# Expert stage: results stored with a partition's four tiles together, the last nine groups by GpSimd through row numbers

## The chip, the cores and the metric

One of the eight cores of a Trainium2 chip runs the program. TensorE multiplies matrices, VectorE (DVE), ScalarE (ACT) and GpSimd (POOL) work on tiles, SyncE (SP) issues DMAs; ACT and POOL issue DMAs too, and all of these run on the core's 16 DMA engines. The metric is the device time of the program in microseconds (us), the median of three runs.

## What is computed

10,000 nodes with 512 features go through two graph layers and two feed-forward layers, each with a layer norm and a residual sum. The change touches the last layer, a mixture of 64 experts in which each node takes two experts:

```
sel = route(x, hash_proj, 2)                # two experts of 64 for each node
pos = place of each (node, expert) pair within its expert; keep = pos < 1250
buf[expert, pos] = x of the kept pairs
h = gelu(buf @ W1[expert])                  # 512 -> 32
y = h @ W2[expert]                          # 32 -> 512
out = mean over the node's two picks of y[expert, pos] * keep
x = x + out
```

## The kernel before, in words

The kernel runs in stages, with a barrier of all engines between them: the projections of the first graph layer (79 tiles of 128 nodes), its edges, its combination with the first feed-forward layer, the edges and nodes of the second graph layer with the routing, the expert stage, and the combine stage. The order of the work is written out by hand for each engine; engines wait for one another by semaphores.

The routing gives every (node, expert) pair a slot, so that an expert's pairs stand together and each expert starts on a new tile of 128 slots. There are at most `LISTED` = 219 such tiles, in `NG` = 55 groups of four (the last has three). How many hold pairs depends on the data; with the given inputs, the choices worked out from the reference fill 188 tiles, 47 groups, and the rest of the list is empty. Slots without a pair have a row number beyond the bound, and the DMA leaves them out.

The expert stage (lines 2081 to 2252) takes the tiles in turn. GpSimd gathers a tile's 128 rows of 2 KB through row numbers into one of eight buffers `xg` (L2122; it waits until the tile eight before has been transposed). TensorE transposes the tile (`turn`, L154), VectorE copies it to `gT` (L2236), TensorE multiplies a group by the up-weights (L2144), ScalarE applies gelu (L2188), TensorE multiplies by the down-weights (L2156), VectorE copies the four results to one of three groups of buffers `yo` (`result`, L2243), and ScalarE's queue stores the group to the tensor `YL` in HBM, "slot_outputs" (`store`, L2193). SP loads the down-weights of each group (L1622); ScalarE copies the up-weights out of `w1all` (L2180), which SP loads at the start of the stage (L2109), behind a store of 128 zero rows (L2108) for which GpSimd clears `zrow` (L2118). VectorE's turn in group g is: copy the tiles of g, then the results of g-2; before the first result of a group it waits until the store that used the buffers three groups ago has landed. After groups 8, 10 and 12 it also works out the slots' row numbers of the first three batches of the next stage (`find`, L2214 to L2230, result `qs`).

In the combine stage (2255 to 2345) GpSimd gathers, for four tiles of 128 nodes at a time (a batch), the two slots' rows of each node out of `YL` (L2295), and VectorE adds them with their weights to the residual (L2334, L2338). VectorE finds the row numbers of a batch three batches ahead (L2311 to L2328); GpSimd waits for them and for the sums of the batch three before.

Of the kernel before, what the change touches and what calls it, by code (L numbers as in the profile page):

```python
# [8 lines left out]
F32 = mybir.dt.float32  # L9
# [28 lines left out]
LISTED = (2 * N + ME * (P - 1)) // P  # L38
DROPPED = 200000.0
# [23 lines left out]
def gnn_ffn(nc, x, xTt, src, dst, Wl, Wr, att, gbias, Wc0, b1c, W2e, b2e, WT, bG, hashp, M1, M2, out):  # L63
    ctx = ExitStack()
    with ctx:
# [32 lines left out]
        FS = nc.dram_tensor("flat_src", [FL + P], F32).ap()  # L98
        RRR = nc.dram_tensor("window_resets", [EP, 2 * P], F32).ap()
# [92 lines left out]
        def unrolled(n, steps):  # L192
# [13 lines left out]
        wl = sb("wl", [P, DK, D], F32, pa)  # L206
        ef = sb("ef", [EP, 2, EC], F32, pa)
# [35 lines left out]
        (c_pool, c_id, c_int, c_ef, c_pad, c_flat, c_win, c_ne, c_rr, c_tab, c_len, c_dg, c_dgm, c_mk, c_mkt, c_tr,  # L243
         c_kd, c_idx, c_st, h_oh, h_mm, h_deg) = (
            sem("i_" + n) for n in ("pool id int ef pad flat win ne rr tab len dg dgm mk mkt tr kd idx st oh mm deg").split())
# [11 lines left out]
        with nc.Block() as block:  # L257
            @block.sync
            def _(sp):
# [21 lines left out]
                sp.wait_ge(c_st, 48)  # L281
                for s in range(4):
                    sp.wait_ge(a_st[s], 16 * len(range(s, NT, 4)))
                    sp.wait_ge(a_sr[s], 16 * len(range(s, NT, 4)))
                    sp.wait_ge(a_sb[s], 16 * len(range(s, NT, 4)))

            @block.scalar
            def _(act):
# [40 lines left out]

                more = ((wc, Wc0), (wg, WT), (hp, hashp), (w2, W2e))  # L330
# [12 lines left out]
            def _(pool):  # L343
# [20 lines left out]
                pool.memset(mk[:], 0.0)  # L364
                pool.memset(zin[:, 0:XE], 0.0)
# [1172 lines left out]
        trow = sb("trow", [1, 4 * P], I32)  # L1538
        ids = sb("ids", [P, 2 * P], I32)
# [45 lines left out]
        idf = sb("idf", [P, 2, P], F32, pe_)  # L1585
        g_c = sem("g_c")
        g_ld, g_t, g_tr, g_rw, g_rw2 = (sem(n) for n in ("g_ld", "g_t", "g_tr", "g_rw", "g_rw2"))
# [36 lines left out]
        with nc.Block() as block:  # L1624
# [106 lines left out]
            def _(dve):  # L1731
# [227 lines left out]
                nc.vector.tensor_copy(trow[:], bank[0][0:1, 0:4 * P]).then_inc(g_rw, 1)  # L1959
                dve.wait_ge(g_ld, 32)  # L1960
# [3 lines left out]
                dve.wait_ge(g_rw, 2)  # L1964
            @block.tensor
# [121 lines left out]
        zrow = sb("zrow", [P, D])  # L2087
# [6 lines left out]
        p_ld, p_st = sems("p_ld", 8), sems("p_st", 3)  # L2094
# [287 lines left out]
```

## Time and profile before

| | |
|---|---|
| median of 3 runs | 2737.44 us (2734.61 to 2737.51) |
| span of the profiled execution | 2733.6 us (3.8 us below the median) |
| busy in the span: PE, DVE, ACT, POOL | 77%, 67%, 36%, 66% |
| expert stage | 2151.6 to about 2504 us |
| combine stage | 2504.6 to the end |

The engines' rows in the trace give a start and a duration; a number of tiles merged into one row is shown as "x4". In brackets stands how long the engine had been idle before, and what ended the wait. "issue" is time in which the engine waited for nothing that the profile shows. The DMA share is the sum of the packets' times over 16 engines, and can pass 1. The granted clock of TensorE is a fraction of 2.4 GHz.

### The profile page before, as it was taken

The numbers are of one execution on the slowest core, as the hardware profiler recorded it, in microseconds if no ns is written. First come the engines' busy times: TensorE is split into PE (matmuls) and PEld (weight loads), VectorE is DVE, ScalarE is ACT, GpSimd is POOL, SyncE is SP. The second block draws the span as 40 slices with busy tenths as digits, with TensorE's granted clock in tenths as the row PEclk, the third lists the DMA queues.
The fourth block names the chain that finished last, engine by engine and source line by source line (L and its number), as shares of the span: only waits on it lengthen the run. The fifth ranks groups of instructions, "written<-read, shape, count | busy, mean of one in ns | idle before, by whom it ended". The sixth has DMA issues, their size and how long they took to land. (4 is left out here: it accounts for less than half of the span.)

```text
span 2733.6 us, 43338 instructions
## 1 busy us (share of the span) xinstructions
PE 2118.0 (77%) x11528; PEld 1261.1 (46%) x11554; DVE 1837.2 (67%) x5188; ACT 988.2 (36%) x2224; POOL 1794.8 (66%) x2144
## 2 busy tenths in 40 slices
PE   8999999957787738999978969999998377774000
PEld 3444444435565526665644426666665244452000
DVE  4776776645555569999951116777777388886675
ACT  1111111115555515777773425555555122220000
POOL 3555555567777458887737755777777667664776
PEclk9999999978999959999999989999999599997555
DMA  5755555548999746888749976666664599996999
GB/s 198 232 190 178 191 184 182 193 147 271 307 314 312 258 154 193 256 260 262 238 180 324 409 285 211 214 220 215 212 214 138 179 342 371 366 338 242 371 383 360
DMA packets 331876, 689.90 MB, mean 252 GB/s; under 512 B 48217, under 2 KB 55347, under 8 KB 331505
## 3 DMA queue, kind: packets, MB, share of 16 engines
q1 hardware_dynamic: 220088, 404.15, 42.7%
q0 software_dynamic: 76720, 218.39, 24.5%
q10 hardware_dynamic: 34825, 64.59, 6.4%
q8 instruction: 96, 1.57, 0.2%
q14 instruction: 147, 1.20, 0.1%
HBM read 416.71 MB, written 287.44 MB: 258 GB/s over the span
## 5 line engine op out<-in xcount | busy, mean ns | idle before, releaser
L2122 POOL DMA_INDIRECT xg<-n_rows,ids x219 | 219.0, 1000 | 109.6 <-PE psum L154 61.6
L148 PE MATMUL psum<-wl,xT 128*128 128x512 f32 x632 | 288.8, 600 | 0.0
L148 PE MATMUL psum<-wg,yT 128*128 128x512 f32 x632 | 285.5, 595 | 0.0
L148 PE MATMUL psum<-wr,xT 128*128 128x512 f32 x632 | 284.1, 592 | 0.0
L337 ACT ACTIVATE xb<-xa,xsc 128x512 f32<-128x512 f32 x79 | 64.2, 814 | 480.3 <-POOL xsc L397 480.3
L384 POOL TENSOR_TENSOR ve<-mv,epst 128x1 f32<-128x1 f32 x79 | 51.1, 647 | 254.1 <-DVE mv L439 254.1
L1688 POOL DMA_INDIRECT slot_tokens<-sl x158 | 169.1, 1070 | 70.9 <-issue 66.9
L2295 POOL DMA_INDIRECT q<-slot_outputs,qs x158 | 167.8, 1062 | 72.3 <-issue 47.8
L154 PE MATMUL psum<-ident,xg 128*128 128x128 f32 x876 | 136.4, 294 | 92.9 <-DVE gT L2236 73.4
L148 PE MATMUL psum<-wc,x1T 128*128 128x264 f32 x632 | 162.8, 402 | 35.0 <-DVE hb L1231 27.4
L148 PEld LDWEIGHTS psum<-wr,xT 128*128 128x128 f32 x632 | 120.1, 190 | 151.2 <-issue 151.2
L1072 POOL TENSOR_TENSOR oc<-ta,ts 128x512 f32<-128x512 f32 x79 | 137.4, 1740 | 59.1 <-DVE ta L1196 31.2
L154 PEld LDWEIGHTS psum<-ident,xg 128*128 128x128 f32 x876 | 99.9, 148 | 161.3 <-issue 138.6
L148 PEld LDWEIGHTS psum<-wl,xT 128*128 128x128 f32 x632 | 115.0, 190 | 120.2 <-issue 120.2
L533 DVE SCALAR_TENSOR_TENSOR xl<-psum,rs,gb_b 128x512 f32<-128x512 f32 x79 | 59.2, 749 | 163.8 <-PE psum L148 163.8
L148 PEld LDWEIGHTS psum<-wg,yT 128*128 128x128 f32 x632 | 114.5, 191 | 114.1 <-issue 114.1
L2236 DVE COPY gT<-psum 128x512 f32<-128x512 f32 x219 | 141.2, 683 | 37.6 <-PE psum L154 37.6
L686 POOL DMA_INDIRECT gl<-xl_rows,idx x118 | 136.7, 1158 | 38.6 <-issue 32.8
L2243 DVE COPY yo<-psum 128x512 f32<-128x512 f32 x219 | 135.8, 682 | 32.5 <-PE psum L2156 26.1
L690 POOL DMA_INDIRECT gr<-xr_rows,idx x118 | 132.9, 1127 | 36.0 <-issue 30.8
L148 PE MATMUL psum<-hp,x3T 128*128 128x256 f32 x632 | 149.9, 380 | 2.5 <-ACT x3T L2046 2.5
L1330 PE MATMUL psum<-w,hT 128*128 128x512 f32 x316 | 148.7, 593 | 0.0
(323 smaller groups left out, 5316.5 us busy)
## 6 DMA issues: line engine op xcount, KB each, us to landing
slot_outputs<-yo ACTq DMA_DIRECT2D x54, 1024.0 KB
x_rows<-x SPq DMA_DIRECT2D x158, 256.0 KB, 3.2
edge_sums<-eo SPq DMA_DIRECT2D x29, 1056.0 KB, 6.5
edge_sums<-go SPq DMA_DIRECT2D x29, 1024.0 KB
xT<-in_xTt SPq DMA_DIRECT2D x79, 256.0 KB
xl_rows<-xl SPq DMA_DIRECT2D x79, 256.0 KB
xr_rows<-xr SPq DMA_DIRECT2D x79, 256.0 KB
residual_rows<-xb SPq DMA_DIRECT2D x79, 256.0 KB, 3.8
```

What stands on the lines that cost most here:

```text
L148: last = nc.tensor.matmul(ps, lhs[:, k, :], rhs[:, k, :], start=(k == 0), stop=(k == DK - 1))
L154: last = nc.tensor.transpose(ps[:, k * P:(k + 1) * P], rows[:, k * P:(k + 1) * P], ident[:])
L337: act.activation(xb[:, s, :], xa[:, s, :], ACT.Identity, scale=xsc[:, s, 1:2], bias=xsc[:, s, 0:1]).then_inc(a_xb, 1)
L686: pool.indirect_dma_start(gl[:, w % 16, :], None, XL, bass.IndirectOffsetOnAxis(idx[:, 0, w:w + 1], 0), bounds_check=NP - 1, oob_is_err=Fa ...
L690: pool.indirect_dma_start(gr[:, w % 8, :], None, XR, bass.IndirectOffsetOnAxis(idx[:, 1, w:w + 1], 0), bounds_check=NP - 1, oob_is_err=Fal ...
L1072: pool.tensor_tensor(oc[:, t % 3, :], ta[:, t % 3, :], ts[:, t % 3, :], ALU.add).then_inc(c_o, 1)
L1330: nc.tensor.matmul(bank[3 + 4 * h], hT[:, h, k, :], w2[:, k, :], start=(k == 0), stop=False)
L1688: pool.indirect_dma_start(IDXF, bass.IndirectOffsetOnAxis(sl3[:, k, t:t + 1], 0), sl3[:, 2, t:t + 1], None, bounds_check=ME * SLOTS * P - ...
L2122: pool.indirect_dma_start(xg[:, t % 8, :], None, XN3, bass.IndirectOffsetOnAxis(ids[:, t:t + 1], 0), bounds_check=NP - 1, oob_is_err=False ...
L2236: nc.vector.tensor_copy(gT[:, t % 8, :, :].rearrange("p k n -> p (k n)"), bank[t % 2]).then_inc(p_T, 1)
L2243: nc.vector.tensor_copy(yo[:, t % 12, :], bank[4 + t % 4]).then_inc(p_y, 1)
L2295: pool.indirect_dma_start(q0[:, b % 3, t % 4, k, :], None, YL, bass.IndirectOffsetOnAxis(qs[:, b % 3, t % 4, k:k + 1], 0), bounds_check=LI ...
```

## The change

The rows of `YL` get another order: the slot of partition p in tile t of group g was row 512 g + 128 t + p, and becomes row 512 g + 4 p + t. So one partition's four results of a group lie side by side, and a group's store has 128 rows of 8 KB where it had 512 of 2 KB. ScalarE's queue stores groups 0 to 45 in this way (`SURE` = 46). The last nine groups are stored by GpSimd, with an indirect DMA of one row number for each partition (`store_wide`); the row numbers `wide` are worked out at the end of the routing, and those of a group that begins behind the last tile in use lie beyond the bound, so that nothing is written. `YL` is declared at the top, the row of zeros moves behind the last group, and the row blocks from group 46 on are filled with zeros in the projection stage, by ten stores on ScalarE's queue. `find` takes the slot number apart with shifts and masks to get the new row, in the expert stage and in the combine stage.

```
--- before
+++ after
+NG = -(-LISTED // 4)
+NOROW = 4 * NG * P
+SURE = 46
...
+                    if 24 <= t <= 24 + 4 * (NG - SURE) and t % 4 == 0:
+                        g = SURE + (t - 24) // 4
+                        n = 4 if g < NG else 1
+                        act.dma_start(YL[4 * g * P:(4 * g + n) * P, :].rearrange("(t p) c -> p t c", p=P),
+                                      zrow[:].unsqueeze(1).to_broadcast([P, n, D])).then_inc(c_zr, 16)
...
+                pool.iota(first[:], [[4, -(-LISTED // 4) - SURE]], base=4 * SURE, channel_multiplier=0,
+                          allow_small_or_imprecise_dtypes=True)
+                pool.iota(where[:], [[P, -(-LISTED // 4) - SURE]], base=P * SURE, channel_multiplier=1,
+                          allow_small_or_imprecise_dtypes=True)
...
+                nc.vector.tensor_scalar(empty[:], first[:], incl[:, ME - 1:ME], None, ALU.is_ge).then_inc(g_em, 1)
+                dve.wait_ge(g_em, 1)
+                nc.vector.scalar_tensor_tensor(wide[:], empty[:], DROPPED, where[:], ALU.mult, ALU.add).then_inc(g_em, 1)
                 dve.wait_ge(g_ld, 32)
                 nc.vector.tensor_copy(idf[:], idr[:]).then_inc(g_t, 1)
...
             def _(sp):
-                sp.wait_ge(z_0, 1)
-                sp.dma_start(YL[LISTED * P:LISTED * P + P, :], zrow[:]).then_inc(z_st, 16)
                 sp.dma_start(w1all[:].rearrange("p e c -> p (e c)"), M1).then_inc(p_all, 16)
...
             def _(pool):
-                pool.memset(zrow[:], 0.0).then_inc(z_0, 1)
+                def store_wide(g):
+                    pool.wait_ge(p_y, tiles(g)[-1] + 1)
+                    pool.indirect_dma_start(YL.rearrange("(r j) c -> r (j c)", j=4),
+                                            bass.IndirectOffsetOnAxis(wide[:, g - SURE:g - SURE + 1], 0),
+                                            yo[:, 4 * (g % 3):4 * (g % 3) + 4, :].rearrange("p j c -> p (j c)"), None,
+                                            bounds_check=NG * P - 1, oob_is_err=False).then_inc(p_sw[g % 3], 16)
+
                 for t in range(LISTED):
...
+                    if t % 4 == 1 and t // 4 - 4 >= SURE:
+                        store_wide(t // 4 - 4)
+                for g in range(NG - 4, NG):
+                    store_wide(g)
...
                 def store(g):
                     n = len(tiles(g))
                     act.wait_ge(p_y, tiles(g)[-1] + 1)
-                    act.dma_start(YL[4 * g * P:(4 * g + n) * P, :].rearrange("(t p) c -> p t c", p=P),
+                    act.dma_start(YL[4 * g * P:4 * (g + 1) * P, :].rearrange("(p t) c -> p t c", p=P)[:, 0:n, :],
                                   yo[:, 4 * (g % 3):4 * (g % 3) + n, :]).then_inc(p_st[g % 3], 16)
...
-                    if g >= 3:
+                    if 3 <= g < SURE + 3:
                         store(g - 3)
...
-                    nc.vector.tensor_scalar_min(qs[:, b % 3, 0:n, :], qg[:, 0:n, :], float(LISTED * P)).then_inc(z_ix, 1)
+                    nc.vector.tensor_scalar_min(qn[:, 0:n, :], qg[:, 0:n, :], float(NOROW)).then_inc(z_n, 1)
+                    dve.wait_ge(z_n, b + 1)
+                    nc.vector.tensor_scalar(qp[:, 0:n, :], qn[:, 0:n, :], P - 1, 2, ALU.bitwise_and, ALU.logical_shift_left)\
+                        .then_inc(z_p, 1)
+                    nc.vector.tensor_scalar(qt[:, 0:n, :], qn[:, 0:n, :], 7, 3, ALU.logical_shift_right, ALU.bitwise_and)\
+                        .then_inc(z_p, 1)
+                    nc.vector.tensor_scalar(qo[:, 0:n, :], qn[:, 0:n, :], 9, 9, ALU.logical_shift_right,
+                                            ALU.logical_shift_left).then_inc(z_p, 1)
+                    dve.wait_ge(z_p, 3 * (b + 1))
+                    nc.vector.tensor_tensor(qp[:, 0:n, :], qp[:, 0:n, :], qt[:, 0:n, :], ALU.bitwise_or).then_inc(z_o, 1)
+                    dve.wait_ge(z_o, b + 1)
+                    nc.vector.tensor_tensor(qs[:, b % 3, 0:n, :], qp[:, 0:n, :], qo[:, 0:n, :], ALU.bitwise_or)\
+                        .then_inc(z_ix, 1)
...
                 def result(t):
                     g = t // 4
-                    if t % 4 == 0 and g >= 3:
+                    if t % 4 == 0 and 3 <= g < SURE + 3:
                         dve.wait_ge(p_st[g % 3], 16 * (g // 3))
+                    if t % 4 == 0 and g >= SURE + 3:
+                        dve.wait_ge(p_sw[g % 3], 16 * len(range(SURE + (g - SURE) % 3, g, 3)))
```

The combine stage's `find` is changed in the same way, and its gathers are bounded by `NOROW`. GpSimd's instructions in the expert stage, before (`xg` is the gathered tile, `n_rows` its source):

```order
L2118 MEMSET zrow 128x512
L2122 DMA xg<-n_rows,ids 128x512 x219
```

and after:

```order
L2153 DMA xg<-n_rows,ids 128x512 x202
L2145 DMA slot_outputs<-yo,wide 7072x2048
L2153 DMA xg<-n_rows,ids 128x512 x4
L2145 DMA slot_outputs<-yo,wide 7072x2048
L2153 DMA xg<-n_rows,ids 128x512 x4
L2145 DMA slot_outputs<-yo,wide 7072x2048
L2153 DMA xg<-n_rows,ids 128x512 x4
L2145 DMA slot_outputs<-yo,wide 7072x2048
L2153 DMA xg<-n_rows,ids 128x512 x4
L2145 DMA slot_outputs<-yo,wide 7072x2048
L2153 DMA xg<-n_rows,ids 128x512
L2145 DMA slot_outputs<-yo,wide 7072x2048 x4
```

The memset is gone; five of the nine wide stores stand between the last 17 gathers, four behind them. VectorE's instructions around the first find of the expert stage, before (`qg` is the slot number, `qs` the row number that GpSimd uses):

```order
L2243 COPY yo<-psum 128x512 x4
L2214 TENSOR_TENSOR qe<-iota,selk 128x512
L2220 TENSOR_TENSOR qj<-qe,cbase 128x512
L2226 TENSOR_REDUCE qf<-qj 128x8
L2228 TENSOR_TENSOR qg<-qf,plk 128x8
L2230 TENSOR_SCALAR qs<-qg 128x8
L2236 COPY gT<-psum 128x512 x4
```

and after:

```order
L2292 COPY yo<-psum 128x512 x4
L2249 TENSOR_TENSOR qe<-iota,selk 128x512
L2255 TENSOR_TENSOR qj<-qe,cbase 128x512
L2261 TENSOR_REDUCE qf<-qj 128x8
L2263 TENSOR_TENSOR qg<-qf,plk 128x8
L2265 TENSOR_SCALAR qn<-qg 128x8
L2267 TENSOR_SCALAR qp<-qn 128x8
L2269 TENSOR_SCALAR qt<-qn 128x8
L2271 TENSOR_SCALAR qo<-qn 128x8
L2274 TENSOR_TENSOR qp<-qp,qt 128x8
L2276 TENSOR_TENSOR qs<-qp,qo 128x8
L2283 COPY gT<-psum 128x512 x4
```

One small operation has become six, ahead of the copies of the next group's tiles.

## Rows read from the trace of the kernel before

**Rows 1.** Windows: us, busy time of PE, PEld, DVE, ACT, POOL, clock, DMA share, GB/s.

```profile
100.00:200.00 100.00, 100.00 (x283) 44.84 (x282) 71.86 (x133) 11.39 (x14) 53.29 (x85) 1.00 0.57 193
2259.00:2441.00 182.00, 139.83 (x1740) 90.83 (x1736) 154.15 (x248) 46.96 (x157) 124.58 (x126) 0.96 1.02 374
```

**Rows 2.** Timeline, VectorE's copies of the results: start us, us, instruction [idle before].

```profile
2259.29 2.48 DVE L2243 COPY yo<-psum 128x512 f32<-128x512 f32 x4 [0.43 <-PE psum L2156]
2264.90 2.48 DVE L2243 COPY yo<-psum 128x512 f32<-128x512 f32 x4 [0.43 <-PE psum L2156]
...
2329.28 2.48 DVE L2243 COPY yo<-psum 128x512 f32<-128x512 f32 x4 [2.90 <-DMA slot_outputs<-yo]
...
2441.49 2.48 DVE L2243 COPY yo<-psum 128x512 f32<-128x512 f32 x4 [1.28 <-PE psum L2156]
```

**Rows 3.** Waits from 2180 to 2440 us: who, for what, total us, times, longest.

```profile
DVE yo L2243 <- DMA slot_outputs<-yo: 6.3, 4, 2.9
PEld psum L154 <- DMA xg<-n_rows,ids: 1.8, 4, 0.8
```

**Rows 4.** DMA queues from 2360 to 2400 us: packets, MB, share of 16 engines.

```profile
q10 hardware_dynamic: 3773, 7.50, 48.6%
q0 software_dynamic: 2243, 6.21, 41.2%
q1 hardware_dynamic: 1436, 1.96, 13.8%
```

**Rows 5.** DMA queues from 2156 to 2166 us, while the up-weights load.

```profile
q1 hardware_dynamic: 183, 3.35, 78.9%
```

**Rows 6.** Timeline of VectorE, the end of one find in the combine stage.

```profile
2541.80 0.17 DVE L2326 TENSOR_TENSOR qg<-qf,plk 128x8 f32<-128x8 f32 x1
2542.00 0.17 DVE L2328 TENSOR_SCALAR qs<-qg 128x8 int32<-128x8 f32 x1
2542.08 2.77 DVE L2334 SCALAR_TENSOR_TENSOR q<-q,w,qx 128x512 f32<-128x512 f32 x4
```

**Rows 7.** Timeline, the start of the expert stage on GpSimd and SP.

```profile
2151.59 0.53 POOL L2118 MEMSET zrow<- 128x512 f32 x1 [6.43 <-POOLq L80]
2152.14 0.33 SPq L2108 DMA_DIRECT2D slot_outputs<-zrow  x1
```

**Rows 8.** Timeline, the end of the expert stage.

```profile
2455.64 1.00 POOL L2122 DMA_INDIRECT xg<-n_rows,ids  x1 [0.30 <-issue]
2457.33 1.00 POOL L2122 DMA_INDIRECT xg<-n_rows,ids  x1 [0.70 <-PE psum L154]
2458.31 2.48 DVE L2243 COPY yo<-psum 128x512 f32<-128x512 f32 x4 [0.43 <-PE psum L2156]
...
2479.76 1.00 POOL L2122 DMA_INDIRECT xg<-n_rows,ids  x1 [0.69 <-PE psum L154]
...
2489.58 0.63 PE L154 MATMUL psum<-ident,xg 128*128 128x128 f32 x4 [1.28 <-DVE gT L2236]
...
2497.75 0.69 DVE L2243 COPY yo<-psum 128x512 f32<-128x512 f32 x1 [0.32 <-PE psum L2156]
2498.47 0.36 ACTq L2193 DMA_DIRECT2D slot_outputs<-yo  x1
```

**Rows 9.** Timeline, small indirect DMAs before the expert stage, and who waits.

```profile
2139.58 0.97 POOL L1688 DMA_INDIRECT slot_tokens<-sl  x1 [0.30 <-issue]
...
2144.15 1.01 POOL L1726 DMA_INDIRECT idr<-slot_tokens,tid  x1 [0.31 <-issue]
...
2146.70 0.29 DVE L1961 CAST idf<-idr 128x256 f32<-128x256 int32 x1 [12.47 <-DMA idr<-slot_tokens,tid]
```

**Rows 10.** GpSimd's gathers of the combine stage: ns min/median/max, waits, and one gather.

```profile
L2295 POOL DMA_INDIRECT q<-slot_outputs,qs x158: 995/1002/1625, 2505.3 to 2719.4; - x158
its engine sat idle before it (us, times) until:
  issue: 47.8, 157
...
2541.50 1.00 POOL L2295 DMA_INDIRECT q<-slot_outputs,qs  x1 [0.30 <-issue]
```

More of the change, by code:

```diff
@@ L206, in gnn_ffn @@
         wl = sb("wl", [P, DK, D], F32, pa)
+        zrow = sb("zrow", [P, D], F32, pa)
         ef = sb("ef", [EP, 2, EC], F32, pa)
@@ L281, in _ @@
                 sp.wait_ge(c_st, 48)
+                sp.wait_ge(c_zr, 16 * (NG - SURE + 1))
                 for s in range(4):
@@ L364, in _ @@
                 pool.memset(mk[:], 0.0)
+                pool.memset(zrow[:], 0.0)
                 pool.memset(zin[:, 0:XE], 0.0)
@@ L1538, in gnn_ffn @@
         trow = sb("trow", [1, 4 * P], I32)
+        wide = sb("wide", [P, -(-LISTED // 4) - SURE], I32)
         ids = sb("ids", [P, 2 * P], I32)
@@ L1585, in gnn_ffn @@
         idf = sb("idf", [P, 2, P], F32, pe_)
+        first = sb("first", [P, -(-LISTED // 4) - SURE], F32, pe_)
+        where = sb("where", [P, -(-LISTED // 4) - SURE], F32, pe_)
+        empty = sb("empty", [P, -(-LISTED // 4) - SURE], F32, pe_)
         g_c = sem("g_c")
-        g_ld, g_t, g_tr, g_rw, g_rw2 = (sem(n) for n in ("g_ld", "g_t", "g_tr", "g_rw", "g_rw2"))
+        g_ld, g_t, g_tr, g_rw, g_em = (sem(n) for n in ("g_ld", "g_t", "g_tr", "g_rw", "g_em"))
         e_ld, e_lx, e_le, e_s3, e_sn, e_id = (
@@ L1964, in _ @@
                 dve.wait_ge(g_rw, 2)
+                dve.wait_ge(g_em, 2)
             @block.tensor
@@ L2078, in gnn_ffn @@
         end_phase(pe_)
-        YL = nc.dram_tensor("slot_outputs", [LISTED * P + P, D], F32).ap()
         qs = sb("qs", [P, 3, 4, 2], I32)
+        qn = sb("qn", [P, 4, 2], I32)
+        qp = sb("qp", [P, 4, 2], I32)
+        qt = sb("qt", [P, 4, 2], I32)
+        qo = sb("qo", [P, 4, 2], I32)
         qe = sb("qe", [P, 4, 2, ME], F32)
@@ L2093, in gnn_ffn @@
         phase.extend(p_w + p_v)
-        p_ld, p_st = sems("p_ld", 8), sems("p_st", 3)
+        p_ld, p_st, p_sw = sems("p_ld", 8), sems("p_st", 3), sems("p_sw", 3)
         p_all, p_cp = sem("p_all"), sem("p_cp")
-        z_eq, z_bs, z_f, z_ix, z_g, z_0, z_st = (sem("z_" + n) for n in "eq bs f ix g 0 st".split())
+        z_eq, z_bs, z_f, z_ix, z_g, z_n, z_p, z_o = (sem("z_" + n) for n in "eq bs f ix g n p o".split())
         p_tr, p_T, p_up, p_h, p_dn, p_y = (sem("p_" + n) for n in "tr T up h dn y".split())
-        NG = -(-LISTED // 4)
         def tiles(g):
@@ L2203, in _ @@
                 for k in range(3):
-                    act.wait_ge(p_st[k], 16 * len(range(k, NG, 3)))
-                act.wait_ge(z_st, 16)
+                    act.wait_ge(p_st[k], 16 * len(range(k, SURE, 3)))
+                    act.wait_ge(p_sw[k], 16 * sum(1 for g in range(SURE, NG) if g % 3 == k))
             @block.vector
@@ L2258, in gnn_ffn @@
         q_ld, q_x, q_st = sems("q_ld", 3), sems("q_x", 3), sems("q_st", 3)
-        q_eq, q_bs, q_f, q_g, q_ix, q_a, q_b = (sem("q_" + n) for n in "eq bs f g ix a b".split())
+        q_eq, q_bs, q_f, q_g, q_ix, q_a, q_b, q_n, q_p, q_o = (sem("q_" + n) for n in "eq bs f g ix a b n p o".split())
         with nc.Block() as block:
@@ L2327, in find @@
                     dve.wait_ge(q_g, b - 2)
-                    nc.vector.tensor_scalar_min(qs[:, b % 3, 0:n, :], qg[:, 0:n, :], float(LISTED * P)).then_inc(q_ix, 1)
+                    nc.vector.tensor_scalar_min(qn[:, 0:n, :], qg[:, 0:n, :], float(NOROW)).then_inc(q_n, 1)
+                    dve.wait_ge(q_n, b - 2)
+                    nc.vector.tensor_scalar(qp[:, 0:n, :], qn[:, 0:n, :], P - 1, 2, ALU.bitwise_and, ALU.logical_shift_left)\
+                        .then_inc(q_p, 1)
+                    nc.vector.tensor_scalar(qt[:, 0:n, :], qn[:, 0:n, :], 7, 3, ALU.logical_shift_right, ALU.bitwise_and)\
+                        .then_inc(q_p, 1)
+                    nc.vector.tensor_scalar(qo[:, 0:n, :], qn[:, 0:n, :], 9, 9, ALU.logical_shift_right,
+                                            ALU.logical_shift_left).then_inc(q_p, 1)
+                    dve.wait_ge(q_p, 3 * (b - 2))
+                    nc.vector.tensor_tensor(qp[:, 0:n, :], qp[:, 0:n, :], qt[:, 0:n, :], ALU.bitwise_or).then_inc(q_o, 1)
+                    dve.wait_ge(q_o, b - 2)
+                    nc.vector.tensor_tensor(qs[:, b % 3, 0:n, :], qp[:, 0:n, :], qo[:, 0:n, :], ALU.bitwise_or)\
+                        .then_inc(q_ix, 1)
                 def combine(b):
```

8 lines of the change are left out of this document (4 added, 4 removed).

## The prediction

> **What bounds the kernel now.** I read the stages in a table of windows first. In the projection stage TensorE is busy 100.00 of 100 us with the DMA at 0.57 of its time; in the middle of the expert stage (2259 to 2441 us) VectorE is busy 154 of 182 us and the DMA share is 1.02 [rows 1]. So the expert stage has two candidates, and the start times of VectorE's copies of the results tell them apart: undisturbed, one group of four tiles follows the last after 5.61 us (2259.29, 2264.90), which is VectorE and TensorE taking turns. Over the 31 groups from 2259.29 to 2441.49 it took 182.2 us, where 31 x 5.61 is 173.9, so 8.3 us went to something else [rows 2]. The list of waits names it: VectorE waited four times, 6.3 us in all, for a store of the results to land, the longest 2.90 us; the rest of the 8.3 us is the slower matmuls behind such a wait. In the same stretch TensorE's weight loads waited 1.8 us for gathered rows, so both streams are at the edge [rows 2, 3].
>
> Why the stores land late: in 40 us of this stretch the queues q10 (stores), q0 (gathers) and q1 (weights) moved 15.67 MB, 392 GB/s, at 103.6% of the engines [rows 4]. One group needs 1.049 MB of stores, 1.049 MB of gathers and 0.262 MB of weights; 2.36 MB at 392 GB/s is 6.02 us against the 5.61 us of compute. The DMA falls behind by 0.4 us a group until a buffer of results isn't free. 31 groups want 186.6 us and took 182.2; the buffers absorbed 4.4 us.
>
> The combine stage is bound by GpSimd: its 158 gathers go out back to back, each after 0.3 us of issue (47.8 us over 157) and nothing else [rows 10].
>
> **The change part by part.**
> Stores of 8 KB rows in place of 2 KB rows, 46 groups. The trace has no 8 KB store. Per MB the engines spent 48.6% x 16 x 40 / 7.50 = 41.5 us on the 2 KB stores and 42.5 us on the gathers [rows 4]; the nearest larger rows are those of the load of all up-weights, 32 KB each: 78.9% x 16 x 10 / 3.35 = 37.7 us [rows 5]. At 37.7, a group falls from 43.5 + 44.6 + 11.8 = 99.9 to 95.9 engine-us, so to 5.78 us; 31 groups want 179.2, less the 4.4 absorbed 174.8: 7.4 us gained. With a fixed cost per row fitted through both sizes (8 ns), 8 KB costs 38.5 us per MB and the gain is 5.8. The ends are 0 (8 KB no cheaper than 2 KB) and 8.3 (no wait left); below 0 is a rival. I take 6.5 us.
>
> The zero row at the start. SP's store of zeros waits for GpSimd's memset, and the 4 MB of up-weights stand behind it on SP's queue [rows 7]. Both go. SP's load goes out up to 0.9 us earlier (the zeros' issue ends at 2152.47, the stage began at 2151.59) and has 256 KB less ahead of it, 0.7 us at 392 GB/s; GpSimd's first gather comes 0.7 us earlier. Between 0.7 and 1.6 us; I take 1.4, since both streams shift.
>
> The row numbers (find), three times in the expert stage. VectorE's step from one small operation to one that needs it is 0.20 us, to one that doesn't 0.08 (2541.80, 2542.00, 2542.08) [rows 6]. Where qs took 0.08 there now stand qn 0.20, qp and qt 0.08 each, qo 0.20, the first "or" 0.20, the second 0.08: 0.84, so 0.76 more. Nothing lies beside it: copies of the next tiles are queued behind, and TensorE waits for these. 3 x 0.76 = +2.3 us; double if the matmuls behind get slower too.
>
> The same in the combine stage, 17 times 0.76 us. VectorE's answer is needed two batches, some 21 us of gathers, later; GpSimd never waits for it now [rows 10], so 0. Without that cover it would be 13 us.
>
> GpSimd's nine wide stores. After gather 201 (2455.64, the 18th from the end) it then waits for the copies of group 46, which end at 2458.31 + 2.48 = 2460.79; gather 202 comes at some 2462.1, 4.8 us late [rows 8]. Then four gathers and a store, 5 x 1.30 = 6.5 us, stand against 5.61: 0.9 later each time, 8.5 us at gather 218, that is at 2488.3 in place of 2479.76. An indirect load lands 2.55 us after its start (2144.15 to 2146.70) [rows 9], so at 2490.8; TensorE turned that tile at 2489.58: 1.3 us late, and the last copy moves from 2498.4 to 2499.7. The last wide store then takes 1.0 and some 1.5 us to land with nothing to write: 2502.3. Now the last plain store goes out at 2498.47, and at 392 GB/s its 0.79 MB with the same 1.5 us end at 2502.0 [rows 8]. So 0, between -2 and +3. Of the nine groups only group 46 holds tokens: the reference's choices fill 188 tiles, 47 groups, so 8 MB are no longer written, in a stretch where the pace is the compute's anyway.
>
> Zeros for ten row blocks, now written in the projection stage: 9.7 MB at 392 GB/s is 25 us of DMA over 37 tiles, beside a TensorE that is always busy and a DMA at 0.57 [rows 1]: 0. Two iotas ahead of the first edge gathers: between 0 and 1.1 us (the memset of rows 7 twice); I take 0.3. The two operations for the wide row numbers stand while VectorE waits 12.47 us for its ids [rows 9]: 0.
>
> Sum: -6.5 - 1.4 + 2.3 + 0 + 0.3 = -5.3 us. The profiled span is 2733.6, so 2728.3; the median of the runs is 3.8 us above the span, which I carry over: 2732 us.
>
> **The rivals.**
> (a) The DMA time isn't saved, or what stores gain the gathers lose. For it: the gathers are already waited for a little [rows 3]. Against: the 32 KB rows are 9% cheaper per byte. The 8.3 us stay, and the time is -1.4 + 2.3 + 0.3 = +1.2, 2738.6; with TensorE's waits for gathers another 3 us, 2742. The Trainium skill (DMA: Bandwidth & Descriptors, Queues, rings and completion order) says that an engine takes turns between the queues packet by packet and drains a whole packet before it switches; by that rule longer rows on the stores' queue take turns from the gathers. No row here shows a store of that size.
> (b) Slower: a wide store keeps GpSimd four times as long, 4.0 us, since its row is four of the usual. First gather 202 is 7.9 us late, then 3.9 more each time, gather 218 at 2503.3 and 16 us late for TensorE; four more stores follow at 4.3 us each, and the stage ends some 21 us later: 2753. It decides from about 1.8 us a store on, where it eats the 5.3 us. Against it: a 4-byte row and a 2 KB row cost the same (0.97 and 1.00) [rows 8, 9].
> (c) The added operations hold up GpSimd's gathers in the combine stage, where each held-up gather adds to the end. Some gathers take up to 1.62 us against a median of 1.00 [rows 10]; at 0.62 for each of 17 batches this is 10.5 us: 2742.5. The gather at 2541.50, in which the old qs fell, took 1.00 [rows 6, 10]. The Trainium skill (SBUF — State Buffer, Who interferes with whom) says that a tensor_scalar in a two-port mode locks GpSimd out for the whole instruction; the trace doesn't show that at this size.
>
> **How the numbers follow.** 0.65 for the forecast, 2728 to 2736; (a) 0.18, (b) 0.10, (c) 0.07. A measurement of this kernel can tell 0.2%, 5.5 us, from no change: below 2732.0 is faster, above 2742.9 slower. The forecast stands at that line: 0.40 faster and 0.25 the same. (a) gives 0.15 same and 0.03 slower, (b) 0.10 slower, (c) 0.02 and 0.05. Together 0.40, 0.42, 0.18. The range goes from all gains at their ends (-8.3 - 1.6 - 2 + 2.3, 2728, less 3 for what shifts with them) to (c): 2725 to 2744; (b) is left out.
>
> **What would show it.** The steps of 5.61 us run through from 2259 us without waits for a store; the stores' engine time per MB is 38 to 39 us; the three finds are 0.8 us longer each; the gathers behind the first wide store come 5 to 9 us late and the stage ends within 2 us of where it does now, less what was gained; the combine stage is as long as before. Wrong is the forecast if waits for gathers take the place of those for stores, if a wide store takes GpSimd much over 1.3 us, or if the combine stage changes by over 3 us.

## The result, and the profile after

The changed kernel took 2749.20 us (median of four runs, 2746.64 to 2753.53), the kernel before 2737.48 us (median of four): a ratio of 1.0043 [1.0030, 1.0057]. In a second set of ten runs it was 2750.72 us, 1.0045 [1.0027, 1.0063]. It is slower, by some 12 us, where 5 us faster were forecast. The profiled span grew from 2733.6 to 2744.9 us, by 11.3 us. That the two profiles reach the expert stage at the same time, so that the differences below add up to it, is luck: across all runs the first results come at 2175 to 2191 us.

To see where, I take the stage between the starts of VectorE's copies of the results: of group 0, 6, 12, 43, 46, and the end of the last copy.

| from, to | forecast | before, us | after, us | difference |
|---|---|---|---|---|
| start of the program to group 0's results | -1.4 + 0.3 | 2180.7 | 2180.6 | -0.1 |
| groups 0 to 6 | 0 | 33.5 | 33.5 | 0.0 |
| groups 6 to 12 (the three finds) | +2.3 | 45.1 | 48.1 | +3.0 |
| groups 12 to 43 | -6.5 | 182.2 | 187.1 | +4.9 |
| groups 43 to 46 | 0 | 16.8 | 17.2 | +0.4 |
| group 46 to the first gather of the combine stage | 0 | 47.0 | 48.25 | +1.3 |
| combine stage | 0 | 228.3 | 230.1 | +1.8 |

Groups 12 to 43 come first. The list of waits of the kernel after, from 2180 to 2440 us (who, for what, total us, times, longest):

```profile
PEld psum L158 <- DMA xg<-n_rows,ids: 31.0, 37, 2.1
PE psum L158 <- DMA xg<-n_rows,ids: 12.1, 15, 1.9
```

VectorE's waits for stores [rows 3] are gone, as forecast, and TensorE's waits for gathered tiles have taken their place: 31.0 us of its weight loads in place of 1.8. VectorE's copies of the results and TensorE's transposes in one held-up group of the kernel after (timeline):

```profile
2332.57 2.48 DVE L2292 COPY yo<-psum 128x512 f32<-128x512 f32 x4 [0.43 <-PE psum L2191]
2332.86 0.66 PE L158 MATMUL psum<-ident,xg 128*128 128x128 f32 x4 [0.38 <-DMA xg<-n_rows,ids]
2334.14 0.66 PE L158 MATMUL psum<-ident,xg 128*128 128x128 f32 x4 [0.63 <-DMA xg<-n_rows,ids]
...
2336.80 0.66 PE L158 MATMUL psum<-ident,xg 128*128 128x128 f32 x4 [0.99 <-DMA xg<-n_rows,ids]
...
2338.64 0.65 PE L158 MATMUL psum<-ident,xg 128*128 128x128 f32 x4 [1.18 <-DMA xg<-n_rows,ids]
...
2341.40 2.48 DVE L2292 COPY yo<-psum 128x512 f32<-128x512 f32 x4 [1.38 <-PE psum L2191]
```

All four tiles of the group come late, and the step is 8.83 us where undisturbed ones are 5.61 [rows 2]. The DMA queues from 2360 to 2400 us of the kernel after (packets, MB, share of 16 engines), against [rows 4]:

```profile
q0 software_dynamic: 2204, 6.09, 45.1%
q10 hardware_dynamic: 937, 6.76, 40.9%
q1 hardware_dynamic: 1336, 1.83, 14.5%
```

The stores (q10) now take 40.9% x 640 / 6.76 = 38.7 engine-us (microseconds of one of the 16 engines) per MB, as forecast (38.5), where they took 41.5. But the gathers rose from 42.5 to 47.4 and the weights from 45.1 to 50.7. Asked for all of groups 12 to 43, the queues say the same: stores 41.9 before and 38.9 after, gathers 45.2 and 48.4, weights 46.0 and 49.4. The windows, against [rows 1] (us, busy time of PE, PEld, DVE, ACT, POOL, clock, DMA share, GB/s):

```profile
100.00:200.00 100.00, 100.00 (x283) 44.86 (x282) 71.75 (x133) 11.39 (x14) 53.15 (x85) 1.00 0.59 202
2262.00:2449.00 187.00, 142.83 (x1740) 90.28 (x1736) 154.94 (x248) 47.01 (x156) 123.45 (x125) 0.96 1.00 362
```

362 GB/s in place of 374. The first row shows the added zeros: 202 GB/s in place of 193, and TensorE busy 100.00 of 100 us as before.

The end of the stage, GpSimd's wide stores (L2145) among its gathers, and TensorE (timeline), against [rows 8]:

```profile
2469.86 1.03 POOL L2145 DMA_INDIRECT slot_outputs<-yo,wide  x1 [5.32 <-DVE yo L2292]
2471.19 1.04 POOL L2153 DMA_INDIRECT xg<-n_rows,ids  x1 [0.31 <-PE psum L158]
...
2476.55 1.09 PE L158 MATMUL psum<-ident,xg 128*128 128x128 f32 x8 [2.41 <-DMA xg<-n_rows,ids]
...
2500.34 0.66 PE L158 MATMUL psum<-ident,xg 128*128 128x128 f32 x4 [1.70 <-DMA xg<-n_rows,ids]
...
2508.59 0.69 DVE L2292 COPY yo<-psum 128x512 f32<-128x512 f32 x1 [0.37 <-PE psum L2191]
2510.06 0.96 POOL L2145 DMA_INDIRECT slot_outputs<-yo,wide  x1 [1.29 <-DVE yo L2292]
```

A wide store costs GpSimd 0.96 to 1.03 us, like a gather; GpSimd stood 5.32 us for the first, and TensorE later waited for late tiles, 2.41 and 1.70 us. One find in the combine stage (timeline of VectorE), against [rows 6], and behind it GpSimd's gathers there (ns min/median/max, and their waits), against [rows 10]:

```profile
2543.89 0.17 DVE L2377 TENSOR_SCALAR qn<-qg 128x8 int32<-128x8 f32 x1
2544.10 0.17 DVE L2379 TENSOR_SCALAR qp<-qn 128x8 int32<-128x8 int32 x1
...
2544.71 0.17 DVE L2388 TENSOR_TENSOR qs<-qp,qo 128x8 int32<-128x8 int32 x1
2544.80 2.73 DVE L2395 SCALAR_TENSOR_TENSOR q<-q,w,qx 128x512 f32<-128x512 f32 x4
```
```profile
L2344 POOL DMA_INDIRECT q<-slot_outputs,qs x158: 994/1000/1627, 2514.8 to 2730.3; - x158
its engine sat idle before it (us, times) until:
  issue: 47.9, 157
```

From qn to the sum it takes 0.91 us, where qs alone stood 0.08 us ahead of it, and the gathers still go out back to back.

### The profile page after: what moved, and what is told of

Read it like the earlier page. It is cut to its first block and busy times, and to the rows that moved or that the text cites. A ratio compares the mean times of both kernels' runs of the same rounds, so it can differ in the third digit from the quotient of the medians.

```text
span 2744.9 us, 43488 instructions
## 1 busy us (share of the span) xinstructions
PE 2124.4 (77%) x11554; PEld 1261.6 (46%) x11554; DVE 1849.3 (67%) x5290; ACT 988.9 (36%) x2224; POOL 1804.4 (66%) x2155
## 5 line engine op out<-in xcount | busy, mean ns | idle before, releaser
L2344 POOL DMA_INDIRECT q<-slot_outputs,qs x158 | 168.6, 1067 | 51.7 <-issue 47.9
L699 POOL DMA_INDIRECT gl<-xl_rows,idx x118 | 136.0, 1152 | 38.6 <-issue 33.7
```

The costliest lines, as they stand in the source:

```text
L699: pool.indirect_dma_start(gl[:, w % 16, :], None, XL, bass.IndirectOffsetOnAxis(idx[:, 0, w:w + 1], 0), bounds_check=NP - 1, oob_is_err=Fa ...
L2344: pool.indirect_dma_start(q0[:, b % 3, t % 4, k, :], None, YL, bass.IndirectOffsetOnAxis(qs[:, b % 3, t % 4, k:k + 1], 0), bounds_check=NO ...
```

## The experiments

Groups are timed in one profile for each run. Theory when I began: the 8 KB rows make the other queues' transfers dearer, which costs groups 12 to 43 about 5 us; the finds cost 3 and the wide stores the rest. Rivals: the row order, not the row length; too few gather buffers; stores and gathers in a bad relation to one another, which another queue would mend; chance, since executions differ by several us. Medians of runs stand beside those of the kernel before on the same chip.

**All groups stored by ScalarE (e1).** Only the wide stores are undone.
```diff
-                    if 3 <= g < SURE + 3:
+                    if g >= 3:
                         store(g - 3)
...
```


> The changed kernel, but ScalarE's queue stores all 55 groups (8 KB rows), GpSimd none. Theory 'turns' (8 KB rows on the stores' queue make the gathers late): the 31 groups between the copies of groups 12 and 43 still take 187 us with TensorE waiting for gathers; only the end of the stage returns to that of the kernel before, so the time falls by 1 to 3 us against the changed kernel, to some 2746 to 2748 us. Theory 'wide stores' (GpSimd's nine stores cost the most): back to within 3 us of the kernel before, 2740 us.

2745.67 us against 2736.31, 1.0042 [1.0026, 1.0058]; groups 12 to 43 took 188.1 us. Group 46 to the first gather of the combine stage took 46.7 us in place of 48.25. So the loss in the middle isn't the wide stores'.

**2 KB rows, the rest as in e1 (e2).** 64 bytes between the result buffers keep the transfer from joining a partition's four tiles; the order of the rows in `YL` stays the changed one.
```diff
-        yo = sb("yo", [P, 12, D], F32, pt)
+        yo = sb("yo", [P, 12, D + 16], F32, pt)
...
-                                  yo[:, 4 * (g % 3):4 * (g % 3) + n, :]).then_inc(p_st[g % 3], 16)
+                                  yo[:, 4 * (g % 3):4 * (g % 3) + n, 0:D]).then_inc(p_st[g % 3], 16)
...
```


> As e1_act_all, but the result buffers are padded by 64 bytes a tile, so that the same bytes go to the same places in rows of 2 KB. Theory 'turns': waits for stores are back, waits for gathers shrink from some 40 to a few us, the 31 groups take 182 us again, and the time is 5 us under e1_act_all, some 2742 us. Theory 'total' (the DMA's total rate decides, whatever the row): 187 us and the time of e1_act_all.

2740.02 us, 1.0020 [1.0009, 1.0031]; groups 12 to 43 took 181.4 us, and VectorE waited 5.9 us for stores, near the 6.3 before. In this profile it is the length of the rows, not their order, that costs the time. The padding isn't what gains it: the kernel before has rows of 2 KB without it, and 182.2 us.

**4 KB rows (e5).** Two tiles side by side.
```diff
-        yo = sb("yo", [P, 12, D], F32, pt)
+        yo = sb("yo", [P, 6, 2 * D + 16], F32, pt)
...
```


> As e1_act_all, but each pair of a group's result buffers is padded by 64 bytes, so that the stores have rows of 4 KB (8 KB there, 2 KB in e2_act_all_2k, same bytes to the same places). Theory 'turns' (a longer row holds an engine longer in the stores' turn): between the two, 183 to 186 us for the 31 groups from 12 to 43 and some 10 to 25 us of waits for gathers. Theory 'one size' (only the 8 KB row does harm): 181 us as with 2 KB.

2742.10 us against 2736.22, 1.0028 [1.0017, 1.0040]; groups 12 to 43 181.9 us, although TensorE's weight loads waited 48.5 us for gathers, longer than in e1. 4 KB rows gain and lose nothing there against 2 KB, the median can't be told from e1's or e2's, and who waits doesn't tell what is lost.

**The same two again (f1 is e1, f2 is e2),** for chance.

> The kernel of e1 (8 KB rows, all groups by ScalarE) once more, for a second profile. Theory row length: the loss belongs to the kernel, and groups 12 to 43 take 186 to 189 us again, with TensorE's waits for gathers over 25 us. Theory chance: single executions of any of these kernels lie between 181 and 188 us, and this one can as well give 181 to 184.

> The kernel of e2 (the same layout, 2 KB rows) once more. Theory row length: groups 12 to 43 take 180 to 183 us again, and the median lies 4 to 7 us under that of the 8 KB rows. Theory chance: anything from 181 to 188 us, and the medians within 2 us of one another.

Groups 12 to 43 took 188.8 (f1) and 183.2 us (f2); medians 2744.83 and 2741.73 us against 2736.61, 1.0019 [1.0003, 1.0036] and 1.0015 [1.0000, 1.0029]. The 5.6 us in the profile came again; the medians lie 3.1 us apart, less than the 4 to 7 I expected, and by these ratios the two can't be told apart. So the cost of the row length is read from the profiles. From the first results to the first gather of the combine stage e1 and f1 took 334.0 and 333.4 us, e2 and f2 327.7 and 328.7. The DMA queues from 2262 to 2440 us of f1:

```profile
q0 software_dynamic: 9319, 25.23, 43.1%
q10 hardware_dynamic: 4191, 30.53, 42.0%
q1 hardware_dynamic: 5613, 7.67, 13.3%
```

The same of f2, with 2 KB rows:

```profile
q10 hardware_dynamic: 15509, 30.79, 45.9%
q0 software_dynamic: 9524, 25.80, 41.1%
q1 hardware_dynamic: 5735, 7.84, 13.6%
```

In engine-us per MB (share x 16 x 178 / MB), stores 39.2 against 42.5, gathers 48.7 against 45.4. The gathers move less than 1.049 MB a group, since slots without a pair are left out: 26.8 MB in the 31 groups of either run, 0.865 MB each. Over exactly these groups the packets' times sum to 99.2% of the engines in f1 and 102.5% in f2, so a group cost 99.2% x 16 x 188.8 / 31 = 96.7 engine-us against 96.9: what the stores gain the gathers and weights lose. The sum of the packets' times also fell, and in this account that is what made the groups longer: 358 against 371 GB/s there. In e1 and e2 it was 97.0 and 96.3 engine-us a group, and 363 against 373 GB/s.

The single packets' records in the traces say how the gathers got dearer. A gather's packets are of 4,096 bytes and typically took as long as before (median 159 ns in the kernel before, 160 in the changed one), but those over 1.3 times the median rose from 9% to 16%, and the mean from 180 to 193 ns. So it is a time of waiting in some packets; whom they wait for the records don't say.

**The changed kernel again (f4).**

> The changed kernel itself once more. Theory row length: groups 12 to 43 take 185 to 188 us, the three finds cost 3.0 us in groups 6 to 12 as in the first profile, and group 46 to the last copy takes 42 to 43 us. Theory chance: groups 12 to 43 anywhere from 181 to 188 us.

Groups 6 to 12 48.0 us, 12 to 43 186.7, group 46 to the last copy 45.0 (2.3 more than in the first profile; TensorE waited 3.28 us for the first tile gathered behind the first wide store, in place of 2.41).

**12 gather buffers with 8 KB rows (e3); with 2 KB rows (e7).**
```diff
-        xg = sb("xg", [P, 8, D])
+        xg = sb("xg", [P, 12, D])
...
```


> As e1_act_all (8 KB rows), with 12 buffers for gathered tiles in place of 8, so that a gather is issued four tiles earlier. Theory 'turns' (gathers late, while the engines' time per byte is lower): with more lead the waits go and the 31 groups come near the compute's 174 to 178 us, 9 to 13 us under e1_act_all, some 2735 us. Theory 'total': the lead is used up once, at most 3 us gained.

> e2_act_all_2k (2 KB rows) with 12 buffers for gathered tiles. With 8 KB rows the four buffers took the 31 groups from 188.1 to 183.6 us. If late gathers come of the 8 KB rows alone, nothing changes here: waits for stores remain, 181 us. If the lead helps at any row length: 176 to 178 us.

e3: 2741.81 us, 1.0023 [1.0011, 1.0035], groups 12 to 43 183.6 us; 4.6 of e1's 6.8 us over e2 came back, more than one theory had it (3) and less than the other (9 to 13). e7: 2738.95, 1.0014 [1.0002, 1.0027], 180.8 us: with 2 KB rows, where VectorE waits for stores, the added buffers bring 0.6 us over e2.

**Stores issued by SP on the weights' queue, 8 KB rows (e6).**
```diff
-                    act.dma_start(YL[4 * g * P:4 * (g + 1) * P, :].rearrange("(p t) c -> p t c", p=P)[:, 0:n, :],
+                    sp.dma_start(YL[4 * g * P:4 * (g + 1) * P, :].rearrange("(p t) c -> p t c", p=P)[:, 0:n, :],
                                   yo[:, 4 * (g % 3):4 * (g % 3) + n, :]).then_inc(p_st[g % 3], 16)
...
```


> As e1_act_all (8 KB rows), but SP issues the stores, on the queue of the weights, and ScalarE's queue is empty: the gathers share the engines with one queue in place of two. Theory 'turns by queue': the gathers get one turn in two in place of one in three, waits for gathers shrink from some 40 us to under 15, waits for stores come back, and the 31 groups take 180 to 183 us in place of 188. Theory 'rate' (the engines move no more bytes in whatever order): 187 to 188 us.

2739.43 us, 1.0010 [0.9996, 1.0025]; groups 12 to 43 185.8 us. TensorE's waits went to 1.3 us and VectorE waited 11.3 us for stores instead. The queue decides who waits; the rate stayed at 356 GB/s. It gave back 2.3 us of e1's middle: 185.8 lies between the two theories' ranges, and 0.9 us under the shortest of five profiles with 8 KB rows on ScalarE's queue. In SP's order the store of a group stands behind the weights of the group six later, so the place of the issue changed with the queue.

**16 gather buffers with 8 KB rows (e9), and with the finds first (e10; f3 is e10 again).** The finds stand ahead of the first copies, in place of after groups 8, 10 and 12:
```diff
+                for b in range(3):
+                    find(b)
...
-                    if g in (8, 10, 12):
-                        find(g // 2 - 4)
```


> The kernel after with all 55 groups stored by ScalarE in 8 KB rows (as in e1) and 16 gather buffers for 8 groups ahead, in place of 8 for 4; the four added ones are cleared by VectorE at the start of the stage. Theory lead: the 8 KB packets only make some gathers late, and with enough of them ahead the DMA engines are never short of work: groups 12 to 43 take 180 to 182 us (as with 2 KB rows, 181.4), the DMA share of 2262:2440 is 1.02 or more, and the waits of TensorE for gathers fall under 10 us. Theory rate: beside 8 KB rows the engines move less in a second whatever stands in their queues: groups 12 to 43 stay at 183 to 185 us, as with 12 buffers (183.6), at 365 to 369 GB/s.

> The same with the three finds of the last groups' place ahead of the groups' copies in VectorE's order, as in e4. Theory lead: groups 0 to 46 take 265 us or less, since the 10 us that the finds cost go and the 180 to 182 us of groups 12 to 43 stay; the time is 2728 us or less. Theory rate: groups 0 to 46 take 267 to 271 us, as e4's 269.2, and the time is 2729 to 2733 us: 8 KB rows bring nothing over e4's 2 KB rows.

> The kernel of e10 (8 KB rows, 16 gather buffers, finds first) once more; its first profile was of its slowest execution (2739.5 against a median of 2730.3). Theory lead: groups 12 to 43 take 180 to 184 us and the median is 2728 to 2732 us. Theory rate: 186 to 188 us again.

e9: 2739.61 us against 2735.13, 1.0020 [1.0004, 1.0035]; groups 12 to 43 181.3 us, as the lead theory had it, though TensorE's weight loads still waited 22.9 us for gathers and the DMA share was 1.00, where it wanted under 10 us and 1.02. e10 and f3: 187.9 and 188.9 us, near the rate theory, with 2730.27 and 2731.86 us, 0.9977 [0.9965, 0.9990] and 0.9975 [0.9961, 0.9988]. Their groups 0 to 46 took 273.8 and 272.9 us, longer than both theories allowed (267 to 271 and 265). The window from 2262 to 2440 us of f3:

```profile
2262.00:2440.00 178.00, 132.11 (x1644) 83.67 (x1642) 146.66 (x235) 44.28 (x146) 117.30 (x118) 0.99 0.99 363
```

Its waits for gathers from 2180 to 2440 us:

```profile
PEld psum L158 <- DMA xg<-n_rows,ids: 34.5, 35, 2.2
```

With 16 gathers in the queue TensorE still waits 34.5 us for them, at 363 GB/s. Both sets fit one reading: the added buffers are a lead that is used up once. With the finds in the middle, VectorE pauses, GpSimd fills the added buffers, and groups 12 to 43 live on them. The queue's bytes in these groups bear it out: gathers moved 26.7 to 26.8 MB in the five profiles with 8 buffers (first profile, e1, f1, f4 and f6, below), 25.7 in e3 and 24.9 in e9 and f5 (below). Eight tiles at 0.216 MB are 1.7 MB, 4.7 us at 372 GB/s by this estimate; against the 187.9 us that the five have in the mean, e3 gained 4.3, and e9 and f5 6.6 and 7.7. With the finds first there is no such pause, and the added buffers gave nothing in groups 12 to 43; they were used before: groups 0 to 12 took 68.7 and 67.2 us in e10 and f3, and 72.3 with 8 buffers (f7, below). More buffers don't raise the rate.

**The kernel before with the finds first (e4), and with 12 gather buffers and 16 result buffers as well (e8).** The same edit as in e10, on the kernel before.

> The kernel before, with the three finds of the expert stage moved ahead of the first copy, where VectorE waits 17 us for its first tile. If the pace of the stage is the compute's, the three steps of 9.0 to 9.7 us become 5.6 and 11.4 us go: 2726 us. If the DMA's rate sets it (6.02 us a group), the 46 groups can't take less than 277 - 4.4 us absorbed = 272.5 in place of 277.6, waits for stores grow, and 5 us go at most: 2732 us.

> The kernel before with the finds first (e4_before_find_first), 12 buffers for gathered tiles and four groups of result buffers in place of three: the two buffers through which a late DMA stops the engines are each one group deeper. The 46 groups took 269.2 us with the finds first, 11 us over the compute's 258. If the waits for stores are a lag that deeper buffers absorb: 260 to 264 us, and 2721 to 2725 us. If the engines' rate bounds the stage: 267 to 269 us and no more than 2 us under e4_before_find_first.

e4: 2729.12 us, 0.9974 [0.9961, 0.9988]; groups 6 to 12 34.2 us in place of 45.1, 12 to 43 184.7. e8: 2728.17, 0.9965 [0.9952, 0.9979], 33.7 and 183.1 us. Both beat both kernels; the buffers add nothing that can be told from e4. By the time of the program e10 and f3, with 8 KB rows and 16 gather buffers, are as good as e4. With the finds first, 12 to 43 is 183.1 and 184.7 us with 2 KB rows and 187.9 to 188.9 with 8 KB.

**16 gather buffers with the wide stores (f5).**

> The changed kernel, its nine wide stores kept, with 16 gather buffers in place of 8. Theory late gathers: a wide store costs by making TensorE's gathers late, as GpSimd stands 5.3 us for group 46's results; with eight more tiles gathered ahead these waits go, and group 46 to the last copy falls from 42.7 and 45.0 us to 39.7 to 40.5 us; the median falls to 2739 to 2743 us (e9's 2739.6 plus the rest). Theory drain: the end of the stage is late because the wide stores themselves stand behind one another on GpSimd; then 42.5 us or more stay. For groups 12 to 43 the lead gives 181 to 184 us, or 186 to 189 us if 16 buffers bring nothing there.

2745.02 us against 2740.39, 1.0015 [1.0001, 1.0030]. Groups 12 to 43 fell to 180.2 us, but group 46 to the last copy stayed at 44.3: I had missed that the store's place among the gathers is fixed. The first wide store (timeline of GpSimd):

```profile
2471.24 1.03 POOL L2151 DMA_INDIRECT slot_outputs<-yo,wide  x1 [16.55 <-DVE yo L2300]
```

GpSimd now stands 16.55 us there, and gather 202 comes as late as before. So this run couldn't tell the theories apart, and its median lies above the 2739 to 2743 us expected.

**Each wide store one group later (f6), and the finds first as well (f7).**
```diff
-                    if t % 4 == 1 and t // 4 - 4 >= SURE:
-                        store_wide(t // 4 - 4)
+                    if t % 4 == 1 and t // 4 - 5 >= SURE:
+                        store_wide(t // 4 - 5)
...
```


> The changed kernel with each wide store one group later among the gathers (group g's behind gather 4(g+5)+1 in place of 4(g+4)+1), so that GpSimd no longer stands 5.3 us for group 46's results; five of them follow the last gather. Theory late gathers: gather 202 goes out with the others, TensorE's waits for gathers at the end of the stage go, and group 46 to the last copy falls from 42.7 and 45.0 us to 39.7 to 41 us; the median falls to 2744 to 2747 us, that of ScalarE's stores (2745.7, 2744.8). Theory count: the nine stores take 1.3 us each of GpSimd, wherever they stand; then 42 us or more stay. Groups 12 to 43 stay at 186 to 189 us, since the rows are still of 8 KB.

> The same with the three finds ahead of the groups' copies: what is left of the change is its 8 KB rows, its zeros and its iotas. If the three costs add up (finds 10 to 11 us with their old place counted, wide stores 2 to 4 us), groups 6 to 12 take 33.6 to 35.2 us, groups 12 to 43 take 187 to 190 us, and the median is 2734 to 2738 us; e4, the kernel before with the finds first, stays 5 us or more below it. If the 8 KB rows cost only in company with the finds' stalls, the median is 2728 to 2731 us.

The first wide store and the last of f6 (timeline):

```profile
2476.50 1.03 POOL L2145 DMA_INDIRECT slot_outputs<-yo,wide  x1 [0.30 <-issue]
...
2513.12 0.96 POOL L2145 DMA_INDIRECT slot_outputs<-yo,wide  x1 [0.83 <-DVE yo L2292]
```

No wait, and group 46 to the last copy took 39.7 us, with the same nine stores: late gathers were the cost. From group 46 to the first gather of the combine stage it took 45.3 us, the kernel before 47.0, the changed one 48.25 and 50.6 (f4). The kernels with 8 KB rows and no wide store took 45.8 to 46.7 there (e1, f1, e3, e6, e9), so even well placed the wide stores gain no more than 0.5 to 1.4 us over ScalarE's. Groups 12 to 43 stayed at 188.6. f6's median, 2748.32 against 2739.21, 1.0032 [1.0014, 1.0050], can't be told from the changed kernel's by its interval, and lies above the 2744 to 2747 expected. f7: 2741.22 us, 1.0010 [0.9994, 1.0027]; groups 0 to 46 took 277.8 us, 8.6 more than in e4, of which 4.6 came before group 12 and 3.7 in groups 12 to 43. The median lies 3 us above what additive costs allowed (the kernel before, too, was 3 us longer on this chip than beside e4) and 10 us above the other theory. With 8 gather buffers the 8 KB rows cost without the finds' stalls too; with 16 the time of the program doesn't show it (e10 and f3 against e4).

## Why the prediction was wrong

**Stores, -6.5 forecast, +4.9 measured: the step that failed.** "At 37.7, a group falls from 43.5 + 44.6 + 11.8 = 99.9 to 95.9 engine-us": I changed the stores' time per MB and left the gathers' and weights' as they were. The stores did fall by as much as I said, and the packets bear out the fixed cost per row: a store's packets of 2, 4 and 8 KB took 84, 159 and 309 ns at the median (kernel before, e5, changed kernel), which is 9 ns and 75 ns for each 2 KB, where I had fitted 8 ns. But a group cost 96.7 and 96.9 engine-us in f1 and f2, and over groups 12 to 43 the packets' times summed to 99.2 to 100.0% of the engines in the five profiles with 8 KB rows named next, where with shorter rows it was 101.3 to 102.9%. Time per MB under load isn't a price that stays when something else changes. The kernel before has it too: at the start of the stage, with no stores on the queues, the gathers cost 73.6% x 160 / 2.17 = 54.3 engine-us per MB (queue q0 from 2165 to 2175 us):

```profile
q0 software_dynamic: 797, 2.17, 73.6%
```

Groups 12 to 43 took 186.7 to 188.8 us in the five profiles with 8 KB rows, 8 gather buffers, ScalarE's queue and the finds in their place (first profile, e1, f1, f4, f6), and 180.8 to 183.2 us in the five with shorter rows (before, e2, f2, e5, and e7 with its 12 buffers). Rival (a) had this mechanism, "what stores gain the gathers lose". It too was too small, 2738.6 to 2742: I priced it as no gain, with at most 3 us of waits for gathers, and it was a loss of 5. The rule of the Trainium skill named there (DMA: Bandwidth & Descriptors, Queues, rings and completion order: an engine drains a whole packet of a queue before it turns to the next) agrees in direction with the gathers' 48.7 against 45.4 engine-us per MB; no run here looked at the turns of an engine, so that this is the cause isn't shown. Nor is it shown why the packets' times sum to less.

A second slip didn't decide, since the forecast gain hardly hangs on it: 3.1 engine-us less a group, on 16 engines and over 31 groups, are 6 us by this estimate. I gave the gathers 1.049 MB a group; the queue moved 0.865. A group is then 2.18 MB, 5.57 us at the 392 GB/s of my 40 us window, less than the 5.61 us of compute: by that sum nothing would have fallen behind. Over groups 12 to 43 the rate was 373 GB/s, and 68.0 MB at that rate are the 182.2 us measured. The "4.4 us absorbed" by the buffers is a product of the two wrong numbers, and no run shows it.

**The finds, +2.3 forecast, +3.0 measured.** Groups 6 to 12 took 47.9 to 48.4 us in all 13 profiles with this find after groups 8, 10 and 12, and 45.1 us before. Each find is longer by 0.76 us, 3.29 in place of 2.53, just as forecast. The first step grows by as much, the second and third by 1.3 and 1.0 us; "double if the matmuls behind get slower too" was the right bound. TensorE's transposes behind the second find show the slowing, and so do the windows of the whole step. Before:

```profile
2235.20 1.23 PE L154 MATMUL psum<-ident,xg 128*128 128x128 f32 x8 [3.73 <-DVE gT L2236]
2229.52:2238.53 9.01, 5.28 (x57) 3.02 (x57) 7.28 (x13) 2.02 (x7) 4.67 (x6) 0.88 1.01 339
```

After:

```profile
2236.68 1.88 PE L158 MATMUL psum<-ident,xg 128*128 128x128 f32 x8 [4.49 <-DVE gT L2283]
2230.24:2240.54 10.30, 5.81 (x58) 3.71 (x58) 8.04 (x19) 2.25 (x8) 4.79 (x6) 0.83 0.87 307
```

TensorE stood idle 0.76 us longer, its granted clock over the step, a mean of its levels of 1.2 and 2.4 GHz, was 0.83 in place of 0.88, and the same eight transposes took 0.65 us more. In the third step the clock was 0.70 in place of 0.82, in the first 0.76 in both. What I didn't ask is what a find costs there at all: e4 takes the three of the kernel before out of the middle, and 10.9 us go from groups 6 to 12, of which 2.5 come back in 12 to 43.

**Wide stores, 0 forecast between -2 and +3, +1.3 measured (f4: +3.6).** GpSimd's wait was forecast at 4.8 us and was 5.3; rival (b), four times the time, is refuted by 1.03 us. The lateness was there too, but TensorE waited already for the first tile behind the store (2.41 us, until 2476.55), not only for the last. That gather went out at 2471.19 and was there 5.36 us later; I had taken 2.55 us for a landing, from a small load before the stage. f6 shows that the place was the whole cost: one group later, and the end is 1.7 us better than before, of which 0.3 to 1.2 us come with the 8 KB rows without any wide store (45.8 to 46.7 us against 47.0).

**The start, -1.4 forecast, 0 measured.** The start of the stage on SP, GpSimd and TensorE in the kernel after (timeline), against [rows 7]:

```profile
2151.19 0.34 SPq L2134 DMA_DIRECT2D w1all<-in_M  x1
2151.89 1.00 POOL L2153 DMA_INDIRECT xg<-n_rows,ids  x1 [7.14 <-POOLq L83]
...
2164.01 1.11 PE L158 MATMUL psum<-ident,xg 128*128 128x128 f32 x4 [16.31 <-DMA xg<-n_rows,ids]
```

The load of the up-weights went out 1.33 us earlier (2152.52 before), the first tile was turned 0.44 us earlier (2164.45 before). Counted from the end of the routing's copy of row numbers to `idf`, which takes out the different starts, the first tile was turned 17.45 us later before and 17.05 after, and the first results came 33.7 us later in both. The windows show where the gain went in this pair of profiles. Of the kernel before:

```profile
2174.00:2175.00 1.00, 1.00 (x18) 0.60 (x11) 0.00 (x0) 0.14 (x1) 0.74 (x1) 0.54 0.75 234
2175.00:2176.00 1.00, 0.89 (x8) 0.65 (x6) 0.51 (x1) 0.45 (x2) 0.26 (x1) 1.00 0.83 322
```

Of the kernel after:

```profile
2174.00:2175.00 1.00, 1.00 (x12) 0.73 (x5) 0.00 (x0) 0.28 (x1) 0.76 (x1) 0.50 0.81 281
2175.00:2176.00 1.00, 0.86 (x6) 0.62 (x4) 0.57 (x1) 0.62 (x2) 0.00 (x0) 0.84 0.74 205
```

TensorE's granted clock is at 1.2 GHz (0.50 from 2165 to 2174 us in both) when the stage begins, and it goes to 2.4 GHz within the two windows shown, later in the kernel after (0.50 and 0.84 against 0.54 and 1.00), though its tiles came 0.4 us earlier. The eight transposes at that moment took 1.58 us there and 1.17 before.

**Combine stage, 0 forecast, +1.8 measured.** Rival (c) is refuted: GpSimd's idle time is 47.9 us over 157 gathers, as before [rows 10]. All profiles of this code lie between 224.5 and 234.3 us, and the 1.8 us is within that.

**Zeros and iotas.** The first results come at 2175 to 2191 us in the profiles of all kernels, the kernels without the zeros among them (2180.7, 2182.3, 2191.1), so a cost of a few us ahead of the expert stage can't be excluded. Nor is the 0.3 us for the iotas shown or refuted by any run. In the projection stage itself TensorE was as busy as before.

## What to carry to other kernels

Where several queues share busy DMA engines, a cheaper transfer of one isn't time won: compare the engine time of all of them over a stretch, and reckon with the others getting dearer, as here. Work put into an engine's stream behind a wait must be placed where what it waits for is already done; here one group later took the whole cost away. The cheapest gain was neither: three small computations in the middle of a critical turn cost 7 us (e4, 2729.12 against 2736.31), and in the wait at the start of the stage they cost little: the first results came 34.5 us after the routing's copy to `idf`, 33.7 in the kernel before, and in e10 and f3, with the longer finds there, 33.5 and 34.3.

## What the runs showed that I had not expected

- Rows of 8 KB on one queue lowered the rate of a mixed stream: over groups 12 to 43 363, 363, 358, 360 and 361 GB/s in the five profiles named above, where the five with shorter rows have 373, 373, 371, 371 and 370; rows of 4 KB did not (371 GB/s, e5). It held on ScalarE's queue and on SP's (358 GB/s in e6), and with 16 gathers queued (359 and 360 GB/s in e10 and f3).
- A stream whose weight loads wait 48.5 us for gathers (e5) can be as fast as one whose weight loads wait 1.6 us for them, and its VectorE 5.9 us for stores (e2): 181.9 and 181.4 us.
- An indirect store of up to 128 rows of 8 KB, which writes in one group of nine, costs GpSimd 1.0 us. It landed in 5.1 us where it wrote, and in 2.1 us in the two empty ones whose landing the trace has.
